# Two-axis attention and Mamba block: x loaded by rows, q, k and v projections as four 64x64 tile products, first layer norm in two parts

## The reference

```python
def _attn(a, sin, cos, ga, ba, gb, bb, Wq, Wkv, Wo, bo):
    q = _ln(a, ga, ba) @ Wq
    k, v = jnp.split(_ln(a, gb, bb) @ Wkv, 2, axis=-1)
    q, k, v = heads(q), heads(k), heads(v)          # 4 heads of 16
    q, k = _rope(q, sin, cos), _rope(k, sin, cos)
    attn = jax.nn.softmax(jnp.einsum('bhid,bhjd->bhij', q, k), axis=-1)
    out = jnp.einsum('bhij,bhjd->bhid', attn, v)     # then heads merged
    return jax.nn.elu(out @ Wo + bo)

xi = attention along j, for each row i               # "the i half"
xj = attention along i, for each column j            # "the j half"
z  = x + (xi + xj) / 2
# then one Mamba-2 layer and a feed-forward on z (unchanged here):
u = layernorm(z); zxbcdt = u @ in_proj_w.T; xBC = silu(causal_conv(xBC))
h = h * exp(dt * A) + dt * x * B;  y = C h + D x     # scan over each sequence
y = rmsnorm(y * silu(z_gate)) @ out_proj_w.T;  then ff, residual, layernorm, fc1, gelu, fc2, residual
```

## Time and profile before

| what | us |
|---|---|
| median of 3 runs | 325.59 |
| lowest and highest run | 323.31 and 329.58 |
| span of the profiled execution | 322.8 |

### The profile page before, as it was taken

One profiled execution on the slowest core, in us unless ns is written; L12 is line 12 of the kernel. 1 busy time (PEld: TensorE's weight loads), 2 busy tenths in 40 slices (PEclk: granted clock), 3 DMA queues, 4 the chain that ended last, 5 costly groups with the idle time before them and its releaser, 6 DMA issues.

```text
span 322.8 us, 7252 instructions
## 1 busy us (share of the span) xinstructions
PE 262.6 (81%) x2802; PEld 141.2 (44%) x2802; DVE 221.4 (69%) x397; ACT 192.2 (60%) x364; POOL 115.4 (36%) x96
## 2 busy tenths in 40 slices
PE   0267999899999999978864799997999849966652
PEld 0131153445565665655653265553445424344321
DVE  2844767976786868799766586899767966385322
ACT  2551264566878888888854933567557346823290
POOL 9230041304041340680040772755796931400000
PEclk9999799999999999999998879998999988997767
DMA  3901101001202021425252500000000000012003
...
DMA packets 29937, 13.77 MB, mean 43 GB/s; under 512 B 26320, under 2 KB 28496, under 8 KB 29904
## 3 DMA queue, kind: packets, MB, share of 16 engines
...
HBM read 3.96 MB, written 2.10 MB: 19 GB/s over the span
## 4 chain that ended last, share of the span: by engine, by line
PE 57%; DVE 19%; ACT 11%; issue 8%; SPq 2%; DMA 1%; DVEq 0%; ACTq 0%
PE bank L501 48%; PE bank L508 10%; DVE mix L1038 2%; DVE ln_s L755 2%; SPq L449 2%; DVE xhat L786 1%; DVE ln_v L771 1%; DVE y_t L1069 1%; DMA x_tok<-x 1%; DVE ln_n L757 1%; DVE cen L759 1%; DVE s_max L960 1%; DVE y_t L1059 1%; DVE x_tok L1064 1%; ACT ln_l L777 1%
## 5 line engine op out<-in xcount | busy, mean ns | idle before, releaser
L1402 POOL TENSOR_TENSOR a_msk<-dt_fin,c_sb 128x512 f32<-128x512 f32 x32 | 39.3, 1228 | 22.8 <-PE bank L501 11.6
L501 PE MATMUL bank<-xn_t,w_att 128*64 128x512 f32 x96 | 41.8, 967 | 2.1 <-DVE v_bd L921 1.7
L501 PE MATMUL bank<-a_msk,c_sb 128*128 128x512 f32 x64 | 36.6, 656 | 0.0
L501 PE MATMUL bank<-k_bd,q_bd 128*128 128x256 f32 x128 | 36.1, 404 | 0.0
L1354 POOL TENSOR_TENSOR k_rot<-rot_cos,rot_swap 128x512 f32<-128x512 f32 x7 | 9.0, 1281 | 73.8 <-DMA rot_swap<-rot_sin 73.8
L1038 DVE TENSOR_TENSOR mix<-dec,g_m 128x512 f32<-128x512 f32 x32 | 31.1, 978 | 2.2 <-ACT dec L1266 1.5
L508 PE MATMUL bank<-c_sb,xhat 128*128 128x128 f32 x48 | 11.0, 367 | 24.7 <-DVE xhat L786 24.6
L960 DVE TENSOR_REDUCE s_max<-bank 128x8 f32<-128x512 f32 x32 | 22.0, 686 | 12.9 <-PE bank L501 12.9
L1186 ACT ACTIVATE prob_t<-bank 128x512 f32<-128x512 f32 x32 | 19.0, 593 | 15.2 <-PE bank L508 15.2
L501 PEld LDWEIGHTS bank<-k_bd,q_bd 128*128 128x128 f32 x128 | 21.7, 189 | 11.8 <-issue 9.3
L1266 ACT ACTIVATE dec<-bank 128x512 f32<-128x512 f32 x32 | 18.9, 591 | 12.2 <-PE bank L501 11.0
...
## 6 DMA issues: line engine op xcount, KB each, us to landing
...
```

The source lines that it names most:

```text
L501: return pe.matmul(dst, lhsT, rhs, start=start, stop=stop, skip_group_check=True)
L1402: gp.tensor_tensor(a_msk[:, m % LAPS, :, :], deep(dt_fin[:, 0, SSM_H * m:SSM_H * (m + 1)], GRID), wide(cst("tri"), SSM_H), ALU.mult).then_ ...
```

## The change

x is loaded twice: first as contiguous rows of 2 KB (row i on partition i, its second half of j on partition 64 + i) on the queues of SP and ACT into `back`, for the first layer norm; later, behind swap(3), as before into `x_tok`. The first layer norm runs in two pairs of quarters, the second between v(0) and its turns. The normalised rows then lie as `xn_j`, with two columns j on the two partition halves, and POOL copies them into a second order, `xn_i`, between rotary(0) and rotary(1). A projection becomes four matmuls of 64 rows by 64 columns on 256 columns each; the two of the lower half rows write the upper half of ring bank 0, the others the lower half of ring bank 1, and the 512 columns across the bank border (`MIDDLE`) are read as one. `ring_plan` makes a k, q or v use wait for what both banks held, and both banks wait for it. The biases are columns `b_att`, made by twelve products of one column, and added in the DVE products and in the v pass. The v pass is two activations. The tables of the i half are laid out for 512 columns; the sine table is signed later. y is written to DRAM by four transfers a chunk. The patterns of `q_sum`, `k_rot` and the wo passes are reordered in place.

```diff
+def ring_plan(order, tail_at):
+
+    side, before, held, turn = [], [], [None, None], 0
+    for r, use in enumerate(order[:tail_at + 2]):
+        if use[0] in ("k", "q", "v"):
+            side.append(0)
+            before.append([u for u in dict.fromkeys(held) if u])
+            held, turn = [use, use], 0
+        else:
+            side.append(turn)
+            before.append([held[turn]] if held[turn] else [])
+            held[turn] = use
+            turn = 1 - turn
+    return side, before
...
+    x_rows = x.rearrange("o i (h j) c -> h (o i) (j c)", h=2)
...
-    turned_w = turned.rearrange("i (u t j) c -> t i u (j c)", t=2, j=2)
+    turned_w = turned.rearrange("i (m g k r) c -> r m g i k c", m=2, g=CHUNKS, r=2)
...
+        ring = ctx.enter_context(nc.psum_tensor("ring", [P, 2 * CW], F32))
+        bank = [ring[:, 0:CW], ring[:, CW:2 * CW]] + [ctx.enter_context(nc.psum_tensor(f"bank{b}", [P, CW], F32)) for b in range(2, 8)]
...
-        xn_t = sb("xn_t", [P, TILES, 2, GRID], att)
+        xn_j = sb("xn_j", [P, TILES // 2, 2, GRID], att)
+        xn_i = sb("xn_i", [P, GRID, TILES], att)
...
-        def xn_cols(d, c, sp):
-
+        def xn_cols(d, c, r, m):
+
+            rows = slice(64 * r, 64 * r + 64)
             if d == 0:
-                flat = xn_t[:, :, :, :].rearrange("p t s (k r) -> p (t s) k r", r=2)
-                return flat[:, :, CT * c:CT * c + CT, sp].rearrange("p i k -> p k i")
-            return xn_t[:, CT * c:CT * c + CT, sp, :]
+                return xn_j[rows, 4 * c:4 * c + 4, m, :]
+            return xn_i[rows, 16 * c + m:16 * c + 16:2, :]
+
+        MIDDLE = ring[:, CW // 2:3 * CW // 2]
+
+        def middle(r):
+
+            return RING[r][:, CW // 2:CW] if r == 0 else RING[r][:, 0:CW // 2]
...
-            for q in range(2):
-                for tau, ip in HALVES:
-                    sp.dma_start(part_of(x_tok, q, tau, ip), x_v[tau, ip, :, 4 * q:4 * q + 4]).then_inc(x_in[q], 16)
-                if q == 0:
-                    sp.dma_start(c_sb[:, :P], consts[:, :P]).then_inc(ident_in, 16)
-            for tau, ip in HALVES:
-                sp.dma_start(x_tok[64 * tau:64 * tau + 64, 8:16, DIM * ip:DIM * ip + DIM], x_v[tau, ip, :, 8:16]).then_inc(x_in[2], 16)
-            sp.dma_start(c_sb[:, P:], consts[:, P:]).then_inc(consts_in, 16)
-            sp.dma_start(l_sb[:, :], cols).then_inc(cols_in, 16)
-            late = po["w_xbc"][0]
+            for a in range(CHUNKS):
+                sp.dma_start(x_rows_of(a)[0:64, :], x_rows[0, :, CW * a:CW * a + CW]).then_inc(xa_in[a], 16)
+                if a == 0:
+                    sp.dma_start(l_sb[:, :], cols).then_inc(cols_in, 16)
+            late = po["cos_i"][0]
             sp.dma_start(p_sb[:, :late], params[:, :late]).then_inc(params_in, 16)
             sp.dma_start(p_sb[:, late:], params[:, late:]).then_inc(late_in, 16)
...
+            for q in range(CHUNKS):
+                for tau, ip in HALVES:
+                    sp.dma_start(part_of(x_tok, q, tau, ip), x_v[tau, ip, :, 4 * q:4 * q + 4]).then_inc(x_in, 16)
             for g in range(CHUNKS):
                 sp.wait_ge(y_turned, g + 1)
-                for tau in range(2):
-                    sp.dma_start(turned_w[tau, :, 4 * g:4 * g + 4],
-                                 y_tok[64 * tau:64 * tau + 64, g, :].rearrange("p (u n) -> p u n", u=4)).then_inc(turned_out, 16)
+                for r in range(2):
+                    for m in range(2):
+                        sp.dma_start(turned_w[r, m, g],
+                                     y_tok[64 * r:64 * r + 64, g, :].rearrange("p (k m c) -> p k m c", k=4, m=2)[:, :, m, :])\
+                            .then_inc(turned_out, 16)
                 swap(CHUNKS + g)
...
-            for q in range(CHUNKS):
+            def turn_rows(q):
+
                 pe.wait_ge(ln_done, q + 1)
                 turn(bank[4 + q], xhat[:, q % 2, :]).then_inc(ln_turned, 1)
-
-            pe.wait_ge(consts_in, 16)
+            turn_rows(0)
             pe.wait_ge(cols_in, 16)
             pe.wait_ge(params_in, 16)
             for d, n in enumerate("ji"):
-                mm(RING[d][64:65, 0:DIM], col(f"ba_{n}"), par(f"wqkv_{n}")[:, 0:DIM])
-                mm(RING[d][64:65, DIM:3 * DIM], col(f"bb_{n}"), par(f"wqkv_{n}")[:, DIM:3 * DIM]).then_inc(bias_row, 1)
-
+                for k, which in enumerate(("ba", "bb", "bb")):
+                    for m in range(2):
+                        rows = slice(64 * m, 64 * m + 64)
+                        last = mm(bank[2][rows, 3 * d + k:3 * d + k + 1], par(f"wqkv_{n}")[rows, DIM * k:DIM * k + DIM],
+                                  col(f"{which}_{n}")[rows, :])
+            last.then_inc(bias_made, 1)
+            turn_rows(1)
...
-                elif r >= 2:
-                    drained(pe, order[r - 2])
+                else:
+                    for held in ring_before[r]:
+                        drained(pe, held)
...
-                    for m in range(2):
-                        last = mm(dst[64 * m:64 * m + 64, :], w_att[d][:, at:at + DIM], xn_cols(d, c, m))
+                    pe.wait_ge(w_scaled, 2 * d + 2)
+                    if d == 0:
+                        pe.wait_ge(xn_ready, c + 1)
+                    else:
+                        pe.wait_ge(xi_ready, CHUNKS)
+                    for r in range(2):
+                        for m in range(2):
+                            last = mm(middle(r)[64 * m:64 * m + 64, :], w_att[d][64 * r:64 * r + 64, at:at + DIM],
+                                      xn_cols(d, c, r, m))
...
-            pe.wait_ge(w_ready, 2)
-            pe.wait_ge(xn_ones, 2)
-            pe.wait_ge(xn_ready, 2 * CHUNKS)
+            pe.wait_ge(consts_in, 16)
             for use in att_steps[-1]:
+                if use == ("vt0", 0):
+                    turn_rows(2)
+                    turn_rows(3)
                 att_use(use)
...
-            for q in range(CHUNKS + 2):
-                if q >= 2:
-                    ln_vector_c(v, q - 2)
-                if 1 <= q <= CHUNKS:
-                    ln_vector_b(v, q - 1)
-                if q < CHUNKS:
-                    v.wait_ge(x_in[q], 64)
+            def ln_rows(first):
+
+                for q in (first, first + 1):
+                    v.wait_ge(xa_in[q], 32)
                     ln_vector_a(v, q)
-            for d in range(2):
-                v.wait_ge(bias_row, d + 1)
-                v.wait_ge(w_scaled, 2 * d + 2)
-                v.tensor_copy(w_att[d][64:65, :], RING[d][64:65, 0:3 * DIM]).then_inc(w_ready, 1)
-            v.wait_ge(sin_signed, 2)
+                for q in (first, first + 1):
+                    ln_vector_b(v, q)
+                for q in (first, first + 1):
+                    ln_vector_c(v, q)
+
+            ln_rows(0)
+            v.wait_ge(bias_made, 1)
+            v.tensor_copy(b_att[:, :], bank[2][:, 0:6]).then_inc(bias_here, 1)
+            v.wait_ge(sin_signed, 1)
+            v.wait_ge(bias_here, 1)
...
-                    for dst, table in ((rot_cos, par("cos_" + "ji"[g // CHUNKS])), (rot_sin, sin_s[g // CHUNKS][:, :])):
-                        v.tensor_tensor(dst[:, slot, :].rearrange("p (t j) -> p t j", j=GRID),
-                                        src[:, :].rearrange("p (t j) -> p t j", j=GRID), wide(table), ALU.mult)\
-                            .then_inc(rotated, 1)
+                    if d == 1:
+                        v.wait_ge(sin_signed, 2)
+                        v.wait_ge(late_in, 16)
+                    bias = b_att[:, 3 * d + 1 - slot:3 * d + 2 - slot]
+                    for dst, table in ((rot_cos, par("cos_" + "ji"[d])), (rot_sin, sin_s[d][:, :])):
+                        v.scalar_tensor_tensor(dst[:, slot, :].rearrange("p (t j) -> p t j", j=GRID),
+                                               MIDDLE.rearrange("p (t j) -> p t j", j=GRID), bias, table_of(d, table),
+                                               ALU.add, ALU.mult).then_inc(rotated, 1)
...
         @block.scalar
         def _(a):
+            for q in range(CHUNKS):
+                a.dma_start(x_rows_of(q)[64:128, :], x_rows[1, :, CW * q:CW * q + CW]).then_inc(xa_in[q], 16)
+                if q == 0:
+                    a.dma_start(c_sb[:, :P], consts[:, :P]).then_inc(ident_in, 16)
+            a.dma_start(c_sb[:, P:], consts[:, P:]).then_inc(consts_in, 16)
             a.preload_act_table_set("natural_log_exp_and_others")
             a.wait_ge(eps_set, 1)
-            for q in range(CHUNKS + 2):
-                if 1 <= q <= CHUNKS:
-                    ln_scalar_b(a, q - 1)
-                if q >= 2:
-                    a.wait_ge(ln_turned, q - 1)
-                    for m in range(2):
-                        a.activation(xn_t[0:64, CT * (q - 2):CT * (q - 1), m, :],
-                                     bank[2 + q][64 * m:64 * m + 64, :].rearrange("p (t j) -> p t j", j=GRID),
-                                     ACT.Identity).then_inc(xn_ready, 1)
```

(36 more changed lines are left out.)

92 lines of the change are left out of this document (57 added, 35 removed).

## The result

| | changed kernel | kernel before, same chip |
|---|---|---|
| median of the runs, us | 330.44 (328.32 to 331.86, 4 runs) | 325.0 (323.31 to 329.58, 4 runs) |
| span of the profiled execution | 329.8 | 322.8 |

The account below looks back on a forecast made before the run. Prediction: TensorE matmul time was the first suspect, strided projections costing more than double. Terms -8.7 - 3.1 + 10.2 + 1.0 - 0.4 = -1.0 gave span 321.8, median 324.6, stated as 324.5 us; range 315 to 332.

Parts of the forecast that it names:

- Part A: Start of the kernel, to the first score: gain 8.7 us, bounds 6 and 10.5, first score at 28.2.
- Part D: Everything else: 1.0 us added (0 to 3) for TensorE's low clock in the first steps; v(7) gives 0.4.
- Part B: The j half, steps 0 to 9: faster projections, gain mostly lost to ring waits; gain 3.1 us, bounds 0 and 7.
- Part C: The i half, steps 10 to 24: waits for rotary products, chunk 16.4, 10.2 us lost, bounds 5 and 13.
- Rival 3: The i half: clock falls to 1.2 GHz in TensorE's gaps, each chunk +4, about 336; chance 0.06.
- Rival 1: Ring waits cost half: C at 5.3 and B at 6, sum -9.8, 315.8; chance 0.25.
- Rival 2: Before rotary(1): POOL's strided copies take 5 us instead of 1.3, price 7.6, time 332; chance 0.09.
- Rival 4: Projections: four tiles run two at a time, each projection about 1.0, +3, 327.6; chance 0.08.
- The signs of what would show it wrong: Chunk 14 us or less; ScalarE awaiting k_rot in step 1; clock under 0.9 from 60 to 130; x after 5.

## Why the prediction was wrong, point by point

**The step that failed is Part A**, the start: -8.7 forecast with bounds 6 and 10.5, -1.4 measured. That is 7.3 of the 8.0 us by which the sum was off; the other stretches miss by -0.2 (B with D), +2.8 (C) and -1.9 (behind step 24), which nearly cancel. Its own steps against the trace, and against the kernel with the value products first, whose start is the same, loads included:

| step of Part A | forecast | measured | same start, other execution |
|---|---|---|---|
| first quarter of x there | 3.2 | 4.73 | 4.72 |
| GpSimd's scalings and sine table ready | 12.1 | 16.70 | 13.94 |
| first product of k begins | 12.4 | 16.73 | 15.09 |
| rotary products of k and q done | 15.8 | 20.8 | 19.2 |
| second pair scaled | 21.8 | 27.9 | 26.2 |
| v_bd done | 24.3 | 31.2 | 29.7 |
| first three sums done | 26.4 | 33.1 | 31.6 |
| first score | 28.2 | 35.5 | 34.0 |

Two terms were taken over from rows that did not fit. The first is the landing of what GpSimd waits for. The forecast took the early parameters for its last input, with 4.6 us to landing; they took 7.2, and 7.1 in the other execution. In the profiled one the last input was another: the constants, issued last on ScalarE's queue at 4.11 and landing 10.0 us later, where they had taken 3.4 before. The text followed the parameters and ScalarE's own work behind the six issues, never when the sixth of them lands. But in the two other executions with this order the constants took 7.2 and GpSimd was ready before the first product; taking the delay away gives only 0.3 to 1.8. The lines of the other execution:
```profile
11.49 0.45 POOL L1424 TENSOR_SCALAR w_att<-p_sb,l_sb 128x64 f32<-128x64 f32 x1 [8.95 <-DMA p_sb<-params]
...
15.09 0.75 DVE L981 SCALAR_TENSOR_TENSOR rot_cos<-ring,b_att,p_sb 128x512 f32<-128x512 f32 x1 [2.09 <-PE ring L546]
```

The second term lies beneath and is there in every execution: the lengths of TensorE's first instructions (1.08 to 1.13 for four transposes or a projection, against 0.60 and 0.66), which Part D priced for the scores and Part A not at all, though the kernel before has them (four turns take 1.09 to 1.12 from 11.17 to 19.60). With x 1.5 us later than forecast, turn, bias products, turn and projection end at 14.9 in the other execution, and its first product waits for TensorE and not for GpSimd. With the constants early the first product still starts at 14.64, not 12.4.

From there on come the order on TensorE (1.6 at the first score, shown by moving the transposes) and VectorE's scalings of the second pair, 2.56 for two beside GpSimd's copies instead of 1.3. The copies, priced at 1.3 and called hidden, took 1.07 to 1.19: rightly priced, wrongly called free. Bias products 1.5, measured 1.44: right. With loads and transposes both moved the first score is at 32.1 to 32.2, still 4 us behind the forecast. By the lengths above that is x (about 1.4), TensorE's slow start (about 2, an estimate from five instruction groups of 0.5 more each, not all on the path) and the scalings (1.2); no run takes these three apart.

**Part B** (-3.1, measured -2.3 with D's share in it) was near, partly by luck: steps 0 to 3 took 12.4 (10.7 forecast), steps 4 to 6 11.3 (14.7) and steps 7 to 9 16.2 (13.7), and these misses nearly cancel. Projections of 0.66 and the two stalls at the fold and at wo(0) were in it. Step 7 was forecast at 7.8 and took 9.1, the slow clock's share: from wo to the next score 3.02, where it is 1.63 at full clock (119.70 to 121.33). Step 6, forecast 8.6, took 5.5, because the late weights take 2 us (50.60 to 52.62) where the forecast carried over about 5 from the earlier trace rows: in the kernel before they stood beside GpSimd's k_rot and q_bd, in the changed one GpSimd was idle.

**Part C** (+10.2, measured +13.0) had the mechanism right, and it is the part that the runs bear out best: the added waits alone give a chunk of 16.92, against 16.4 forecast and 16.72 found. Of the 2.8 us over the forecast 1.6 are one slow stretch around step 16, a chunk of 17.77 and one of 17.24, and 1.0 are three chunks of 16.72 instead of 16.4. The three-operand products took 0.74, not 0.68: 0.12 of the 0.15 and 0.19 that the k and q steps run over.

**Part D** put 1.0 on the clock. What is seen is the start and two falls, around steps 7 and 15: about 1.4 us behind wo in step 7 and 1.3 in step 8 (4.09, against 2.82 in the kernel with the scales at step 9), and around step 15 the 1.6 above. One term for the first two steps does not hold them. Rival 3 (the clock falls throughout the i half, 336) did not happen: with waits of 1.3 to 1.7 us the clock is 1.00 from 80 to 100 and from 120 to 140, and 0.68 only from 100 to 105.

**The rivals.** Rival 1, ring waits at half cost (5.3 in the i half), is refuted by the kernel that has them alone (11.9 there, 7% in all); its sum of -9.8 also leaves out Part D's 1.0, with which it is -8.8 and 316.8. Rival 2, GpSimd's copies at 5 us, by their 1.07 to 1.19. Rival 4 by 0.66 a projection. The signs of what would show it wrong were also named: x landing after 5 (4.73, near), a clock under 0.9 between 60 and 130 (it came, at 65 to 75 and 100 to 105). The other two did not come: no chunk is near 14, and ScalarE's wait in step 1 is for TensorE. Behind step 24 the code is unchanged, but the stretch is 191.8 long instead of 194.1, and 190 to 201 in the other kernels; why was not tried. A difference of 2 us between two spans can lie there alone.

On the ring, the Trainium skill (TensorEngine Tiling (Array Packing), section Gotcha 1: PSUM Pressure) says that different row tiles write to different PSUM banks and cannot access the same bank at the same time. This change keeps them apart, and a ring of two banks becomes one for every projection; +2.96 us a chunk is what that cost here. No run tried both row tiles in one bank.
